# A graph network's edge sums: 8 own slots a chunk and 3 shared ones, in alternating pairs of PSUM banks

## The reference

```python
mask = (adj > 0.0)
xj_proj = x @ W1a
diff = x[:, :, None, :] - x[:, None, :, :]
h = relu(xj_proj[:, :, None, :] + diff @ W1b + b1)     # (b, j, k, 192)
hm = einsum('bjkh,bjk->bjh', h, mask)
out = hm @ W2 + deg[..., None] * b2
```

## Time and profile before

| | |
|---|---|
| median of 3 runs | 1898.67 us (1897.78 to 1899.13) |
| the profiled execution | 1900.7 us, of which 1899.0 is the span |
| layer 0's edge work within the span | from about 57 to 1373 us |
| PE busy | 1679.3 us, 88% |
| DVE busy | 1344.1 us, 71% |
| ACT, POOL busy | 974.1 us (51%), 600.4 us (32%) |

### The profile page before, as it was taken

The page is one execution under the profiler, slowest core; times in us unless marked ns, Lnnn a source line. Parts: engine busy times, 40 slices in busy tenths (PEclk is TensorE's granted clock), DMA queues, the critical chain, the costliest instruction groups (busy, mean ns, idle before and its releaser), DMA issues. The chain is left out here.

```text
span 1899.0 us, 49116 instructions
## 1 busy us (share of the span) xinstructions
PE 1679.3 (88%) x13581; PEld 1277.4 (67%) x13582; DVE 1344.1 (71%) x3728; ACT 974.1 (51%) x2265; POOL 600.4 (32%) x706
## 2 busy tenths in 40 slices
PE   1899999999999899999999999899899998994399
PEld 0676666666667676666767666677688897960276
DVE  5688887877888778788877878788734444457633
ACT  2555554545554555554545555454155554745555
POOL 0343433434434444434433334344300000026300
PEclk9999999999999999999999999999989998997699
DMA  5000000000000000000000000000000000000011
GB/s 120 7 12 7 7 6 6 6 6 12 6 6 6 6 8 10 6 6 6 6 6 8 10 6 6 6 0 1 1 0 0 0 0 1 0 0 0 11 40 39
DMA packets 40222, 18.57 MB, mean 10 GB/s; under 512 B 18792, under 2 KB 40106, under 8 KB 40106
## 3 DMA queue, kind: packets, MB, share of 16 engines
q1 hardware_dynamic: 39574, 17.28, 3.8%
q10 hardware_dynamic: 532, 0.21, 0.1%
HBM read 13.29 MB, written 4.19 MB: 9 GB/s over the span
## 5 line engine op out<-in xcount | busy, mean ns | idle before, releaser
L532 PE MATMUL bank<-ac_lo,work 128*128 128x192 f16 x2495 | 528.6, 246 | 0.0
L532 PE MATMUL bank<-ac_hi,work 128*128 128x192 f16 x2495 | 528.6, 246 | 0.0
L781 POOL TENSOR_TENSOR acc<-acc 128x384 f32<-128x384 f32 x256 | 267.2, 1065 | 734.3 <-DVE acc L738 734.3
L726 DVE SCALAR_TENSOR_TENSOR acc<-bank,acc 128x384 f32<-128x384 f32 (+1 forms) x1060 | 466.0, 494 | 12.5 <-PE bank L532 6.6
L524 PE MATMUL bank<-ac_hi,ident 128*128 128x384 f16 (+1 forms) x1060 | 326.7, 308 | 89.6 <-DVE acc L726 48.0
L702 DVE TENSOR_SCALAR work<-work,slot_key 128x896 f16 (+2 forms) x393 | 271.7, 691 | 90.5 <-issue 88.3
L524 PE MATMUL bank<-ac_lo,ident 128*128 128x384 f16 (+1 forms) x1060 | 324.4, 306 | 0.0
L532 PEld LDWEIGHTS bank<-ac_lo,work 128*128 x2495 | 244.0, 98 | 68.3 <-issue 0.2
L532 PEld LDWEIGHTS bank<-ac_hi,work 128*128 x2495 | 243.8, 98 | 68.4 <-issue 0.2
L637 ACT ACTIVATE hmTa<-bank,unscale 128x128 f32<-128x128 f32 x128 | 47.1, 368 | 444.9 <-PE bank L496 444.9
L524 PEld LDWEIGHTS bank<-ac_hi,ident 128*128 128x128 f16 x1060 | 103.3, 97 | 174.4 <-DVE acc L735 91.2
(11 more groups left out here) (204 smaller groups left out, 3129.4 us busy)
## 6 DMA issues: line engine op xcount, KB each, us to landing
adj_in<-in_adj_dram SPq DMA_DIRECT2D x32, 256.0 KB, 2.9
out_dram<-acc SPq DMA_DIRECT2D x32, 128.0 KB, 2.0
l1w<-in_L_gnn_W_dram SPq DMA_DIRECT2D x2, 64.0 KB
l1b<-in_L_gnn_b_dram SPq DMA_DIRECT2D x2, 64.0 KB
x_all<-in_x_dram SPq DMA_DIRECT2D x4, 0.2 KB, 11.7
nm_in<-in_nodemask_dram ACTq DMA_DIRECT2D x1, 64.0 KB
w1a<-in_L_gnn_W_dram ACTq DMA_DIRECT2D x1, 48.0 KB
w1b<-in_L_gnn_W_dram ACTq DMA_DIRECT2D x1, 48.0 KB
```

What stands on the lines that cost most here:

```text
L532: last = nc.tensor.matmul(ps[:, t * H:(t + 1) * H], hot, part[:, q, H:2 * H], start=False, stop=(e == 1 and t == slots - 1))
L726: nc.vector.scalar_tensor_tensor(out=sums, in0=bank[n_bank][:, 0:slots * H], scalar=0.0, in1=sums, op0=ALU.min, op1=ALU.add).then_inc(s_fr ...
L781: last = nc.gpsimd.tensor_tensor(t[:, 0:2 * H], t[:, 0:2 * H], t[:, 2 * H:4 * H], ALU.add)
```

## The change

- A chunk has 8 own slots in place of 7, a shared chunk 3 in place of 5, with the constants that follow (`NC`, `DIV`).
- Four of the PSUM banks are one tensor, `slot_banks`, seen as two pairs. A slot takes 256 columns' room, so a pair holds four slots: half a chunk. Halves alternate between the pairs, across graphs also: five units a graph, the shared slots being the fifth.
- VectorE sums a half in one operation over 768 columns (`dve_half`, new L745), and cuts the shared slots in one of 576 (L779). TensorE waits for the pair as a whole.
- The first own chunk is written out ahead of the inner loop, so the loop's body stands twice on TensorE.
- The one-hot ring has two places, and the shared one-hot its own. The one-hot of the next chunk is made after the first half of the present one is summed. `acc2` is double.
- The first sum of a graph adds to `pads` (192 columns, ScalarE) in place of a started `acc`. GpSimd no longer reads the count.
- On VectorE the counting work moves behind the shared cut (`after`), and the x update, now of the graph three back, before the last own sum (`halfway`).
- VectorE's outer loop asks for a prefetch of the loop's start (`hint_back_edge`).

```diff
-    OWN = [(0, 0, 0, 2), (1, 1, 2, 2), (2, 5, 4, 2), (3, 6, 6, 1)]
-    SHARED = [(0, 0, 0, 2), (1, 1, 2, 2), (3, 6, 4, 1)]
-    SC = 7
-    SS = 5
+    SU = 4
+    SC = 2 * SU
+    SS = 3
+    SB = 2
+    SW = 256
...
-    NC = MAXR - MINC - 1
+    NC = MAXR - MINC
...
-    DIV, SH = 13108, 16
-    RING = 4
+    DIV, SH = 21846, 16
...
-        onehot = place(RING * CH)
+        onehot = place(2 * CH)
+        onehot2 = place(SS * N)
...
+        def pe_seeds(pair, count, node, q):
+
+            for t in range(0, count, SB):
+                n = min(SB, count - t)
                 for e, part in enumerate((ac_hi, ac_lo)):
+                    nc.tensor.matmul(unit(pair, t, n), node, part[:, q, 0:H].unsqueeze(1).broadcast_to([N, n, H]),
                                      start=(e == 0), stop=False)
...
+        def pe_half(pe, k, q, at, cnt):
+
+            pair = (q + k) % 2
+            pe_seeds(pair, SU, ident16[:, :], q)
+            if k == 0:
+                pe.wait_ge(s_G, cnt)
+            pe_gathers(pair, SU, lambda t: onehot[:, ds(at + (k * SU + t) * N, N)], q).then_inc(s_done[k], 1)
...
+            at = next_chunk()
+            if not (known(b) and b == 0):
+                pe.wait_ge(s_free[1], prev)
+            pe_half(pe, 0, q, at, cnt)
+            if not (known(b) and b == 0):
+                pe.wait_ge(s_free2, b)
+            pe_half(pe, 1, q, at, cnt)
+            with pe.Fori(0, n):
+                at = next_chunk()
+                pe.wait_ge(s_free[0], prev)
+                pe_half(pe, 0, q, at, cnt)
+                pe.wait_ge(s_free[1], prev)
+                pe_half(pe, 1, q, at, cnt)
             between()
             pe.wait_ge(s_host, g + 1)
-            pe_chunk(pe, q, SHARED, host[:, u, q * N:(q + 1) * N], regs)
+            pe.wait_ge(s_free[0], cnt)
+            pe_seeds(q % 2, SS, host[:, u, q * N:(q + 1) * N], q)
+            pe.wait_ge(s_G2, b + 1)
+            pe_gathers(q % 2, SS, lambda t: onehot2[:, t * N:(t + 1) * N], q).then_inc(s_done2, 1)
...
-            with eng.Fori(1, NI - 1) as i:
+            with nc.Fori(1, NI - 1, engines=bass.OrderedEngineSet([eng.engine]),
+                         hint_back_edge=prefetch_back_edge) as i:
...
+        def dve_half(k, q, first):
+
+            sums = acc[:, q, :].rearrange("p (t h) -> p t h", t=SU)
+            before = pads[:, q, :].unsqueeze(1).broadcast_to([N, SU, H]) if first else sums
+            nc.vector.scalar_tensor_tensor(out=sums, in0=unit((q + k) % 2, 0, SU), scalar=0.0, in1=before,
+                                           op0=ALU.min, op1=ALU.add).then_inc(s_free[k], 1)
...
+            dve.wait_ge(s_done[0], cnt)
+            dve_half(0, q, True)
+            with dve.Fori(0, n) as c:
+                dve_onehot(dve, rs[:, u, q, :, :], c + 1, pos)
                 dve.reg_mov(prev, cnt)
                 dve.reg_add(cnt, cnt, 1)
...
+                dve.wait_ge(s_done[1], prev)
+                dve.wait_ge(s_free[0], prev)
+                dve_half(1, q, False)
+                dve.wait_ge(s_done[0], cnt)
+                dve.wait_ge(s_free[1], prev)
+                dve_half(0, q, False)
+            halfway()
+            dve_shared_onehot(dve, g, u, q)
+            dve.wait_ge(s_done[1], cnt)
+            dve.wait_ge(s_free[0], cnt)
+            dve_half(1, q, False)
...
+            if not (known(b) and b < 2):
+                dve.wait_ge(s_hm, b - 1)
+            dve.wait_ge(s_done2, b + 1)
+            nc.vector.tensor_scalar(acc2[:, q % 2, :].rearrange("p (t h) -> p t h", t=SS), unit(q % 2, 0, SS),
+                                    0.0, None, ALU.min).then_inc(s_free2, 1)
+            after()
```

More of the change, by code:

```diff
@@ L408, in gnn_stack_kernel, with unit @@
         s_bn0 = sem("layer1_stats_made")
-        pT, pU, pSmall = bank[2][:, 0:2 * N], bank[7][:, 0:F], bank[7][:, F:F + GS * NC]
-        pA3, pDeg, pH, pAC = bank[3], bank[4], bank[4], bank[2]
+        pT, pU, pSmall = bank[6][:, 0:2 * N], bank[7][:, 0:F], bank[7][:, F:F + GS * NC]
+        pA3, pDeg, pH, pAC = bank[5], bank[4], bank[4], bank[6]
+        def unit(pair, first, count):
+            return slots[:, pair * SU * SW:(pair + 1) * SU * SW].rearrange("p (t c) -> p t c", c=SW)[:, first:first + count, 0:H]
         def known(v):
@@ L529, in pe_chunk, with pe_gathers @@
[L529 to L534, removed]
-        def pe_slots(pe, b, g, u, q, regs, between):
+        def pe_gathers(pair, count, hot, q):
+            for t in range(count):
+                for e, part in enumerate((ac_hi, ac_lo)):
+                    last = nc.tensor.matmul(unit(pair, t, 1), hot(t), part[:, q, H:2 * H].unsqueeze(1),
+                                            start=False, stop=(e == 1 and (t % SB == SB - 1 or t == count - 1)))
+            return last
@@ L537, in pe_slots @@
             pe.wait_ge(s_lo, b + 1)
             pe.wait_ge(s_n, g + 1)
[L539 to L542, removed]
+            n = pe.value_load(chunks[0:1, ds(b, 1)], min_val=1, max_val=NC + 1)
+            at = next_chunk()
+            if not (known(b) and b == 0):
+                pe.wait_ge(s_free[1], prev)
@@ L710, in count @@
                 dve.reg_mov(prev, cnt)
                 dve.reg_add(cnt, cnt, 1)
[L712 to L737, removed]
-                        nc.vector.scalar_tensor_tensor(out=sums, in0=ps, scalar=0.0, in1=sums,
-                                                       op0=ALU.min, op1=ALU.add).then_inc(s_free[k], 1)
@@ L796, in _ @@
             def _(pe):
[L797 removed]
+                regs = [pe.alloc_register(f"pe_{r}") for r in ("own_chunk", "own_chunk_before", "onehot_place")]
                 pe.reg_mov(regs[0], 0)
@@ L881, in _ @@
                 regs = [dve.alloc_register(f"dve_{r}")
-                        for r in ("chunk", "chunk_before", "own", "own_before", "ring_place", "slot_chunks")]
+                        for r in ("own_chunk", "own_chunk_before", "onehot_place", "later_chunks")]
                 dve.reg_mov(regs[0], 0)
@@ L902, in between @@
                                 dve_first_rows(dve, nxt, p)
-                        if not (known(b) and b < 2):
-                            dve_update(dve, b - 2)
-                    dve_slots(dve, b, g, u, q, regs, between)
-                all_iterations(dve, step)
-                for b in range(B - 2, B):
+                    dve_slots(dve, b, g, u, q, regs, halfway, after)
+                all_iterations(dve, step, prefetch_back_edge=True)
+                for b in range(B - 3, B):
                     dve_update(dve, b)
```

127 lines of the change are left out of this document (56 added, 71 removed).

## The result

The changed kernel takes 2065.85 us (median of 4 runs, 2065.04 to 2067.72) where the kernel before takes 1898.5: a ratio of 1.088 (95% interval 1.086 to 1.090). It is 167 us **slower**; 1807 was forecast. The profiled execution's span is 2066.0 us against 1899.0.

The account below looks back on a forecast made before the run. TensorE was taken to set the pace in the edge work, losing only waits for VectorE. 21 us less work plus 128 x (0.95 - 0.40) = 71 us less waiting made 92 us off 1898.7: 1807 us, range 1780 to 1860.

Parts of the forecast that it names:

- Part 3: New waits of TensorE for bank pairs each freed by one VectorE sum: 0.40 us a graph, bounds 0.1 and 0.95.
- The walk around this term: Timing of one graph on VectorE and TensorE: waits of 0.5 us after q=1, 0.45 after q=2, mean 0.24.
- Part 1, fewer slots: TensorE's gathers: 2432 slots, 63 fewer, so 21 us less work, 0.16 us a graph.
- Part 2, VectorE's work: VectorE's sums: one over 768 columns takes 0.95 us; VectorE gains 0.8 us a graph, off the path.
- Part 3, the one-hot: VectorE's one-hot of chunk 2, now behind the first sum, may meet GpSimd: 0 to 0.4 us, taken as 0.16.
- Part 4, the loop's turn: VectorE's outer loop: the prefetch hint removes the gap at all 13 turns; without it 16 us are lost.
- At nothing: Priced at zero: ScalarE's changed copies and pads, the x update one graph later; GpSimd has 0.5 us less a graph.
- Only the work goes: Rival: pair-wide wait and late one-hot on TensorE's path take back all waiting saved; 1878 us, chance 0.11.
- the hint does nothing: Rival: the prefetch hint on VectorE's outer loop has no effect, 16 us back; 1823 us, chance 0.05.
- The loop no longer fits: Rival: TensorE's loop of some 1550 instructions is reloaded, 3.6 us at 13 turns, +47; 1854 us, chance 0.08.
- Slower: Rival: GpSimd's lock delays each chunk 2 one-hot, sums longer; waiting 1.35 us a graph, +30, 1929 us, chance 0.06.

Follow-up runs that it names:

- e1: The changed kernel with the counting work moved back ahead of the shared cut, all else as changed: 1779.95 us, ratio to before 0.938.
- e2: The changed kernel with GpSimd's four sums of a graph cut to one column each, VectorE's order as changed: 1848.4 us (one run).
- e9: e6 without the prefetch hint on VectorE's outer loop: 1767.88 us, ratio to before 0.931.
- e7: e1 with each own half summed by two operations over 384 columns, the second freeing the pair: 1787.47 us (one run).
- e10: e1 with the one-hot of the second chunk issued ahead of the first own sum: 1775.64 us (one run).
- e5: e1 without the prefetch hint on VectorE's outer loop: 1775.76 us.
- e8: The kernel before with the prefetch hint on VectorE's outer loop and nothing else: 1885.32 us, ratio to before 0.994.
- e6: e1 with product L491 put ahead of the transposes of the next adjacency at q = 0: 1770.53 us.
- e3: The kernel before with its counting work and x update moved behind the three shared sums: 2264.58 us.
- e4: The changed kernel with only the counting work of q = 2 moved back ahead of the shared cut: 1898.87 us (one run).
- e11: The changed kernel with only the counting work of q = 1 moved back ahead of the shared cut: 1933.69 us (one run).

## Why the prediction was wrong

**The step that failed is one term of Part 3**: "Behind it now stands the small work that stood ahead of the shared sum: 1.9 us after q = 1 and 2.1 us after q = 2". Those lengths are right for the place at which they were read the earlier trace rows, where GpSimd is quiet: its operations begin at 641.74 and the last, at 645.03, is 0.92 us long, while the small work stands at 648.20. At the new place, behind the operation that releases GpSimd's sums, they are 3.82 and 4.63 us. The text of the prediction had the timing in hand ("GpSimd's sums begin after the shared cut, at about 1.3 ... to about 5") and used it for the one-hot alone, though the small work stands in front of the one-hot in that very time. Its place made it long: e1 puts back the place alone and e2 takes away GpSimd's length alone, and each gives back over 200 us.

**The walk around this term held.** With the lengths forecast it gave waits of 0.5 and 0.45 us. Put in the measured lengths, and the extra goes straight to the wait: 0.5 + (3.82 - 1.9) = 2.4 and 0.45 + (4.63 - 2.1) = 3.0; measured 2.4 and 2.95. In e2, 0.5 + (2.53 - 1.9) = 1.1; measured 1.2. After q = 0, which the walk left at nothing with a work of 1.1 us, 2.48 brings 1.05. A mean wait of 1.6 us a graph in place of 0.24 is 174 us, before the clock.

**The second miss is a term put at nothing without a reason**: the prediction took 2.4 GHz for the whole of the edge work, since the kernel before was granted it. Its longest wait was 1.8 us, at 13 places. What long waits do to the clock was not asked, and it is 78 us here. The forecast was 259 us too low: waiting of 1.75 us a graph by the starts (224 us) in place of 0.40 is 173 of them, the clock 78.

Point by point, the rest:
- *Part 1, fewer slots:* right in the counts (2432, 1024). Its 21 us have no run of their own; e9, with next to nothing left to wait for, has done its edge work at 1241 us, 9.25 us a graph with the start and the end, and 9.21 between 100 and 1150 us, where the prediction's work of 9.31 less 0.16 makes 9.15.
- *Part 2, VectorE's work:* right. The sum over 768 columns was extrapolated to 0.95 us and takes 0.954, so two banks in one operation cost no more than their columns. e7 shows that splitting it loses 7.5 us.
- *Part 3, the one-hot:* 0.16 us a graph was assumed, 20 us in all; e10 gives at most 4.
- *Part 4, the loop's turn:* the gap went, but not by the hint: e5 shows no gap without it. That it went was right by luck. The hint's worth was priced at 16 us; in the kernel before it is 13 (e8).
- *At nothing:* ScalarE's copies hid as assumed, but for those at q = 0, some 9 us, which e6 takes away; the x update a graph later costs one wait of 1.7 us in e1, at the loop's end, and none of that size in e5.

**The rivals.** *Only the work goes* and *the hint does nothing* gave 1878 and 1823 and are out. *The loop no longer fits* is out: TensorE has no gap at its turns, and q8 brings 20 packets, not many more, none of them from 300 to 1200 us. The prediction looked at q8 only; q14, which it left aside, is the one that shows a loop being loaded again in the kernel before. *Slower* had the sign, and the right cause by name, GpSimd's lock, at the wrong operation: it was placed on the one-hot and on longer sums, with 30 us, a fifth of what came. The sums did not get longer, and the one-hot is hardly hit: in the changed kernel it is lengthened after q = 0 alone, to 0.88 us, and its mean is 0.524. The small work stood in this rival at its unhindered length too.

**Left open.** What exactly makes the clock fall: long waits go ahead of it, two kinds together far more often than one. The 10 us of the balance that are not placed. Why e3 loses more than the change. Why e10's order is 4 us better than e1's, and e5 better than e1: both differences are near what can be measured.

## What to carry to other kernels

An operation's length belongs to the place at which it was read. Before a piece of VectorE's work is moved, lay GpSimd's timeline over the new place: if the operation just ahead of it releases GpSimd, each short SBUF operation in it can be as long as a GpSimd operation. Move such work ahead of the release, and put what PE waits for first behind it. And when a walk says that waits grow to 2 us and more, price the granted clock as well.

## What the runs showed of the hardware

- An operation on 4 columns took 0.77 us beside GpSimd and 0.17 alone; one on 56 columns with two inputs in SBUF 1.05 and 0.22. A chain of short operations suffers: the work of 2.2 us became 4.6. The long ones end as a GpSimd operation does, and about every second operation passes unhindered. A reduction (0.21 us) and sums that read PSUM (0.95 us) kept their length beside GpSimd.
- Some 49 stretches of about 3.2 us at 1.2 GHz followed waits of 2.4 and 2.95 us that started 13 us apart, in matmuls that had been at 2.4 GHz. Without the other kind, 2 of 29 waits of 2.4 us (e4) and 12 of 31 of 2.95 us (e11) were followed by one. The waits of 1.2 us in e2, some 60, were followed by none.
- VectorE went back over a loop of some 500 instructions with a gap of 2.8 to 3.6 us, and with the hint 0.55; over one of some 340 with 0.28 to 0.31, hint or none. With the long loop the queue q14 brought 65 instruction packets in 900 us, with the short one none. TensorE went back over some 1550 with no gap.
- One VectorE operation over two PSUM banks, 768 columns, took 0.954 us, as 0.545 us for 384 and 0.342 for 192 had it.
